# Four of sixteen attention tiles of each group transposed by VectorE and device memory instead of TensorE

## The reference

```python
q, k, v = (proj(Wq), proj(Wk), proj(Wv))
scores = jnp.einsum('bhsd,bhtd->bhst', q, k) * scale
scores = jnp.where(mask[None, None, :, :], -jnp.inf, scores)
attn = jax.nn.softmax(scores, axis=-1)
out = jnp.einsum('bhst,bhtd->bhsd', attn, v)
out = out.transpose(0, 2, 1, 3).reshape(B, S, E)
out = out @ Wo.T
rms = jnp.sqrt(jnp.mean(out * out, axis=-1, keepdims=True) + EPS)
xn = out / rms * rms_scale
...
xn = xn * (1.0 + sc[:, None, :]) + shift[:, None, :]
...
x = x + _L0_cond_ref(x, mask_SxS_bk1, cond_256, ...)
x = x + _L1_cond_ref(x, cond_256, L1_cond_q_right, L1_cond_spectral_gate)
```

## Time and profile before

| what | value |
| --- | --- |
| median of three runs | 858.3 us (858.19 to 858.86) |
| span of the profiled execution | 855.4 us, so 2.9 us less than the median |
| TensorE busy | 846.5 us (99%) |
| VectorE busy | 628.7 us (73%) |
| ScalarE busy | 615.9 us (72%) |
| GpSimd busy | 482.5 us (56%) |
| chain that ended last | PE 97%, DVE 1%, issue 1%, ACT 1% |

### The profile page before, as it was taken

How to read it: one execution, slowest core, us unless ns; L and a number is a source line. 1 busy time by engine, 2 the same in 40 slices (tenths; PEclk the granted TensorE clock), 3 DMA queues, 4 the chain that set the end, 5 groups by cost and what they waited for, 6 DMA issues and landing times.

```text
span 855.4 us, 17179 instructions
## 1 busy us (share of the span) xinstructions
PE 846.5 (99%) x5344; PEld 640.8 (75%) x5344; DVE 628.7 (73%) x1524; ACT 615.9 (72%) x1504; POOL 482.5 (56%) x346
## 2 busy tenths in 40 slices
PE   9999999999999999999999999999999999999997
PEld 6788888888887777767777677776777767777774
DVE  5521321322338899999999999999999999999886
ACT  6232332232329899999999999999999999999882
POOL 0999990000000111666777667776677766777794
PEclk9999999999999999999999999999999999999999
DMA  8854644654599658786687775788668777569201
GB/s 288 339 212 164 233 172 184 220 185 183 182 284 272 138 112 231 173 203 147 149 204 162 157 207 135 156 185 209 143 148 204 164 160 207 131 157 245 68 26 51
DMA packets 82355, 153.76 MB, mean 180 GB/s; under 512 B 8520, under 2 KB 9160, under 8 KB 82272
## 3 DMA queue, kind: packets, MB, share of 16 engines
q1 hardware_dynamic: 82128, 152.49, 65.8%
q10 hardware_dynamic: 144, 0.26, 0.1%
HBM read 102.35 MB, written 50.36 MB: 179 GB/s over the span
## 4 chain that ended last, share of the span: by engine, by line
PE 97%; DVE 1%; issue 1%; ACT 1%; POOL 0%; DVEq 0%; ACTq 0%
PE banks L788 26%; PE banks L120 14%; PE banks L816 13%; PE banks L851 10%; PE banks L471 9%; PE banks L473 9%; PE banks L472 9%; PE banks L797 2%; PE banks L831 1%; PE banks L456 1%; PE banks L444 0%; DVE probs L685 0%; ACT turned_probs L1013 0%; PE banks L510 0%; DVE banks L955 0%
## 5 line engine op out<-in xcount | busy, mean ns | idle before, releaser
L137 ACT ACTIVATE probs<-probs,least 128x512 f32<-128x512 f32 x512 | 363.4, 713 | 0.0
L129 DVE CUSTOM_DVE_ANT_0 probs<-banks,mask_bias 128x512 f32<-128x512 f32 x512 | 330.0, 681 | 37.5 <-PE banks L120 37.5
L788 PE MATMUL banks<-ident,probs 128*128 128x128 f32 x2048 | 306.4, 272 | 0.8 <-DVE turned_probs L901 0.7
L788 PEld LDWEIGHTS banks<-ident,probs 128*128 128x128 f32 x2048 | 252.6, 140 | 56.7 <-ACT probs L137 2.0
L120 PE MATMUL banks<-k_rows,q_rows 128*128 128x512 f32 x496 | 236.2, 478 | 0.0
L901 DVE COPY turned_probs<-banks 128x512 f32<-128x512 f32 x256 | 175.5, 686 | 2.3 <-PE banks L788 2.3
L400 DVE SCALAR_TENSOR_TENSOR late<-banks,late 128x512 fp32r<-128x512 f32 x64 | 43.9, 690 | 158.7 <-ACT late L337 158.7
L1013 ACT ACTIVATE turned_probs<-banks 128x512 f32<-128x512 f32 x256 | 147.1, 587 | 17.0 <-PE banks L788 13.5
L685 POOL TENSOR_TENSOR late<-rot,late 128x2048 f32<-128x2048 f32 x28 | 129.2, 4615 | 0.0
L337 ACT ACTIVATE late<-banks 128x512 fp32r<-128x512 f32 x64 | 38.2, 598 | 119.6 <-PE banks L473 112.5
L816 PE MATMUL banks<-turned_probs,v_sb 128*32 128x512 f32 (+1 forms) x1088 | 117.0, 570 | 1.3 <-ACT turned_probs L1013 1.3
(11 more groups left out here) (134 smaller groups left out, 1263.0 us busy)
## 6 DMA issues: line engine op xcount, KB each, us to landing
q_rows<-q_scratch SPq DMA_DIRECT2D x128, 256.0 KB, 6.1
k_rows<-k_scratch SPq DMA_DIRECT2D x124, 256.0 KB, 6.5
q_scratch<-late SPq DMA_DIRECT2D x64, 256.0 KB, 2.3
k_scratch<-late SPq DMA_DIRECT2D x64, 256.0 KB, 2.3
v_sb<-v_scratch SPq DMA_DIRECT2D x8, 1024.0 KB, 11.4
out<-late SPq DMA_DIRECT2D x29, 256.0 KB, 7.5
raw<-in_xT SPq DMA_DIRECT2D x7, 1024.0 KB, 5.4
v_scratch<-v_out SPq DMA_DIRECT2D x28, 256.0 KB, 2.0
```

Of the source, the lines that this page charges most:

```text
L129: dve.tensor_tensor_reduce(self.probs[:, n % RING, :], self.ps[:, n % SCORE_BANKS, :], self.mask_bias[:, c, :], 1.0, 3e38, ALU.add, ALU.mi ...
L137: act.activation(self.probs[:, n % RING, :], self.probs[:, n % RING, :], ACT.Exp, bias=self.least[:, n % 32:n % 32 + 1], scale=-1.0, accum ...
L788: last = pe.transpose(turn_bank("tile", n)[:, j * P:(j + 1) * P], probs[:, n % RING, j * P:(j + 1) * P], ident[:, :])
```

## The change

The four tiles of head 0 (places 0 to 3) of each whole group are no longer turned by TensorE. VectorE transposes their 32 x 32 blocks from `probs` into a new tile `blocks` (`block`, at places 0 to 3). SyncE writes `blocks` to device memory in four DMAs of 256 KB, each from 32 partitions, and reads them back in four DMAs, each into 128 partitions of `turned_probs` (`move_blocks`). The first of the four products of each part of `values` reads and writes in a pattern of 32 columns. The moves of the other twelve tiles are dealt out anew: 8 to ScalarE, as before, 4 to VectorE instead of 8. `rescale` and `residual` of VectorE become one step, which reads the projected chunk, the factor and the gain, and GpSimd gets a new step `add`. q and k pieces are loaded into every fourth partition. The ring `probs` has 10 places instead of 12, the `MASKS` and `EXPS` tables stay.

```diff
-RING, SLOTS = 12, HG + 1
+RING, SLOTS = 10, HG + 1
...
+BLOCK_PLACES = (0, 1, 2, 3)
+BLOCKS_AT = (0, 1, 2, 3)
...
-BY_ACT = {'early': '0101010101010101', 'whole': '0101010101010101', 'half': '01010011'}
+BY_ACT = {'early': '----101101101101', 'whole': '----101101101101', 'half': '01010011'}
...
-RESIDUAL = {(m + NG + 1, 1 if m < CHUNKS - 3 else 3): m for m in range(CHUNKS - 1)} | {(V - 1, 6): CHUNKS - 1}
...
     def load_q(self, sp, u, r):
-        sp.dma_start(f32(self.q[r * D:(r + 1) * D, u % 2]),
+        sp.dma_start(f32(self.q[r::HG, u % 2]),
...
-        if n >= RING:
-            dve.wait_ge(self.turned, n - RING + 1)
+        if n >= RING and BY_ACT[n - RING] == "-":
+            dve.wait_ge(self.blocked, n - RING + 1 - TURNS[n - RING + 1])
+        elif n >= RING:
+            dve.wait_ge(self.turned, TURNS[n - RING + 1])
...
+            def move_blocks(v):
+                sp.wait_ge(blocked, TC * (v + 1))
+                if v >= 2:
+                    sp.wait_ge(moved, 16 * TC * (v - 1))
+                for a in (0, 2, 1, 3):
+                    sp.dma_start(scr["blocks"][v % 2, a].rearrange("(k p) t -> p k t", p=D),
+                                 blocks[a * D:(a + 1) * D].rearrange("p k j c t -> p k (j c t)")).then_inc(blocks_out[a], 16)
+                if v >= 2:
+                    sp.wait_ge(valued, v - 1)
+                for a in (0, 2, 1, 3):
+                    sp.wait_ge(blocks_out[a], 16 * (v + 1))
+                    sp.dma_start(turned_probs[:, HG * v % SLOTS, a, :], scr["blocks"][v % 2, a]).then_inc(moved, 16)
...
+                if chunks == ALL:
+                    move_blocks(v)
                 if u + 2 < U:
                     load_unit(u + 2)
...
-                    last = pe.matmul(value_ps[i * D:(i + 1) * D, cols], v_sb[:, b % 2, part, h * D:(h + 1) * D],
-                                     turned_probs[:, (HG * u + i) % SLOTS, part, cols],
+                    to, of = value_ps[i * D:(i + 1) * D, cols], turned_probs[:, (HG * u + i) % SLOTS, part, cols]
+                    if i == 0 and chunks == ALL:
+                        if part == 0:
+                            pe.wait_ge(moved, 16 * TC * (v + 1))
+                        to = to.rearrange("p (c a t) -> p a c t", c=TC, a=TC)
+                        of = turned_probs[:, HG * u % SLOTS, :, part * P:(part + 1) * P].rearrange(
+                            "p a (c t) -> p a c t", c=TC)
+                    last = pe.matmul(to, v_sb[:, b % 2, part, h * D:(h + 1) * D], of,
                                      start=(part == 0), stop=(part == TC - 1))
...
-                turn(n)
+                if BY_ACT[n] != "-":
+                    turn(n)
...
+            def block(n):
+                v, u, i, c = ORDER[n]
+                dve.wait_ge(exped, n + 1)
+                if n == 0:
+                    dve.wait_ge(projected, (TC + 2 * NG) * (B - 1) + 2 * NG)
+                for a in range(TC) if c == 0 and v > 0 else ():
+                    dve.wait_ge(blocks_out[a], 16 * v)
+                dve.transpose(blocks[:, :, :, c, :].rearrange("p k j t -> p j k t"),
+                              probs[:, n % RING, :].rearrange("p (j k t) -> p j k t", j=TC, k=TC)).then_inc(blocked, 1)
...
-                dve.tensor_tensor(scaled[:, :], y_of(m), mod[:, b % 2, E:], ALU.mult).then_inc(scaled_ready, 1)
-
-            def residual(m):
-                c = m % TC
-                dve.wait_ge(scaled_ready, m + 1)
                 dve.wait_ge(rstd_ready, m + 1)
-                dve.wait_ge(shifted, m + 1)
-                dve.scalar_tensor_tensor(x_of(m), scaled[:, :], rstd[:, c % 2:c % 2 + 1], x_of(m),
-                                         ALU.mult, ALU.add).then_inc(summed, 1)
+                if m >= 2:
+                    dve.wait_ge(stored[c % 2], 16 * (m // 2))
+                dve.scalar_tensor_tensor(acc[:, c % 2], y_of(m), rstd[:, c % 2:c % 2 + 1], mod[:, b % 2, E:],
+                                         ALU.mult, ALU.mult).then_inc(scaled_ready, 1)
...
+                if chunks_of(v) == ALL and t in BLOCKS_AT:
+                    block(FIRST[v] + BLOCK_PLACES[BLOCKS_AT.index(t)])
...
+            def add(m):
+                pool.wait_ge(scaled_ready, m + 1)
+                pool.wait_ge(shifted, m + 1)
+                pool.tensor_tensor(x_of(m), x_of(m), acc[:, m % 2], ALU.add).then_inc(summed, 1)
...
+                if v > NG:
+                    rms(v - NG - 1)
                 if 0 < v <= POOL_GROUPS:
                     spread_inverse(v - 1)
                 if v > NG:
-                    rms(v - NG - 1)
+                    add(v - NG - 1)
```

More of the change, by code:

```diff
@@ L32, with tiles_of_group @@
 V = len(GROUPS)
-ORDER = [(v, u, i, c) for v, (u, chunks) in enumerate(GROUPS) for i in range(HG) for c in chunks]
+BLOCK_PLACES = (0, 1, 2, 3)
+BLOCKS_AT = (0, 1, 2, 3)
+def tiles_of_group(chunks):
+    tiles = [(i, c) for i in range(HG) for c in chunks]
+    if chunks == ALL:
+        blocked, tiles = tiles[:TC], tiles[TC:]
+        for place, tile in zip(BLOCK_PLACES, blocked):
+            tiles.insert(place, tile)
+    return tiles
+ORDER = [(v, u, i, c) for v, (u, chunks) in enumerate(GROUPS) for i, c in tiles_of_group(chunks)]
 SIZE = [HG * len(chunks) for _, chunks in GROUPS]
@@ L603, in attention @@
         turned_probs = sb("turned_probs", [P, SLOTS, TC, S])
+        blocks = sb("blocks", [P, TC, TC, TC, D])
         inv = sb("inv", [P, HG, TC])
@@ L631, in attention @@
         valued, normed = sem("valued"), sem("normed")
+        blocks_out = [sem(f"blocks_out{a}") for a in range(TC)]
+        moved = sem("moved")
         o_hi_ready, o_ready = sem("o_hi_ready"), sem("o_ready")
@@ L689, in attention @@
         rows.last_k = values_and_k[:, 0]
-        late_mix = [probs[:, 4 * j:4 * j + 4, :] for j in range(3)]
+        late_mix = [probs[:, 4 * j:4 * j + 4, :] for j in range(2)] + [blocks[:, :, :, :, :].rearrange(
+            "p k j c t -> p k (j c t)")]
+        late_junk = probs[:, RING - 1, 0:E // 2].bitcast(BF16)
         late_out = [turned_probs[:, 3, j, :] for j in range(3)]
@@ L984, in _ @@
                     split_lo(v - 1)
-                if not by_act(n - 1) and n > 0:
+                if n > 0 and BY_ACT[n - 1] == "0":
                     move_out(n - 1)
```

64 lines of the change are left out of this document (33 added, 31 removed).

## The result

The changed kernel takes 901.93 us (median of four runs, 901.3 to 902.49) against 858.25 us of the kernel before: a ratio of 1.0511, with a 95% interval of 1.0497 to 1.0526. It is slower by 5.1%. The forecast was 900.

What follows compares the result with a forecast made beforehand. TensorE sets the pace, with ScalarE's own list also closing the 17.82 us period. Whole groups add 39.0 and 3.0, so 855.4 + 42 = 897, plus 2.9 around it: 900 us; own range 880 to 912, 8 in 10 874 to 936.

Steps and rivals of the forecast that it cites:

- The pace: Whole groups: two transposes before `norm` delay mask 9, exponential 9 and moves 4 and 6; period 19.32 us against 17.82.
- side case without the transposes in the way: Whole groups, transposes at nothing: mask 9 ready at 6.8, exponential 9 at 7.55, turn 6 at 8.3, period 18.1 us.
- about 2 us before the value products: TensorE in whole groups: a wait of about 2 us before values, ended by ScalarE's last move.
- The rest of the period: ScalarE from move 6 on: 7 exponentials, single and paired moves and the square, 9.16 us, no mask or turn late.
- 26 x 1.50 + 3 x 1.0: Added time of whole groups: 1.50 us each for groups 4 to 29, 1.0 each for groups 1 to 3; +42 us.
- 17.5 us is the least that a period could take: ScalarE in whole groups: 16.6 us of work plus the 0.86 us wait before `inv_T`.
- 0, bounded by 1.4 us: Group 0 and the four half groups: no added time, bounded by group 0's four turns, 1.4 us either way.
- `rescale`'s wait for `rms`: VectorE: waiting for GpSimd's `rms` costs nothing, as VectorE waits for score 8 anyway, about 2.6 us after the change.
- Block transposes: VectorE: 0.60 us each, like a copy; rival 1, twice that (1.2): period 20.5, +78, 936 us, chance 0.10.
- The cover in the changed kernel: Blocks through device memory: last read lands at 16.1, values need them at 19.5, so 3.4 us of cover.
- one to two us over the period at worst: q and k loads, if at 205 GB/s: 10 us instead of 5, DMA total 20 us; case then dropped.
- Faster: Rival 3, whole groups: exponential 9 before 7.25, no wait before move 6; ScalarE's 17.5 us period, -10, 848 us, chance 0.11.

Runs made afterwards that it cites:

- each half of it, undone alone: On the changed kernel, either all block transposes moved ahead of mask 8 (867.15 us), or the blocked tiles spread to places 0, 2, 4, 6 (871.57 us).
- both parts undone: Changed kernel with all block transposes ahead of mask 8 and blocked tiles at places 0, 2, 4, 6: 849.38 us, ratio 0.9912 to the kernel before.
- the two runs without blocks: Changed kernel with all sixteen tiles turned by TensorE again: 861.92 us; the same with the residual again in VectorE's two steps: 857.35 us.
- a mean period of 16.90 us: Kernel with all transposes ahead of mask 8, blocked tiles 0, 2, 4, 6, and exponential 7 moved ahead of `inv_T`: 840.45 us, ratio 0.9800.
- the run with spread tiles: Changed kernel with blocked tiles at places 0, 2, 4, 6 instead of 0 to 3, transposes left where they were: 871.57 us, ratio 1.0170.

## Why the prediction was right, and where it was off

**The pace.** Right. The prediction put score 8, mask 8, mask 9 and exponential 9 at 4.21, 4.90, 7.32 and 8.06 in the period, and the trace has them at 4.20, 4.90, 7.31 and 8.04. Moves 4 and 6 were put at 7.07 and 10.16 with waits of 0.68 and 0.69 before them; they stand at 7.10 and 10.18, with 0.61 each. The experiments show the cause, in that each half of it, undone alone, gives 1.2 us per period. The prediction's side case without the transposes in the way, exponential 9 at 7.55, is what the run with all transposes ahead of mask 8 has: 7.54. TensorE's idle time came out in another place than it said: not about 2 us before the value products but 0.64 there, 1.00 before score 12, 0.47 before turn 15 and 0.28 before score 11.

**The rest of the period.** 9.16 us from move 6 on was too much: from 516.48 to the next group's exponential 2 at 525.41 it is 8.93. The square takes 0.57 (505.25 to 505.82), and I had taken 0.68, which is the distance from the square to the move behind it less that move's wait. The two pairs of moves take 1.02 and 0.96 instead of 1.05 each. So the term "26 x 1.50 + 3 x 1.0" was mis-sized: it measured 26 x 1.24 + 3 x 1.09 = 35.4 us, not 42. The same error is in "17.5 us is the least that a period could take": with both parts undone the period is 17.12, of which 0.81 is the wait before `inv_T`, so ScalarE's own work is 16.3 us and not 16.6.

**What was costed at nothing.** Group 0 and the half groups "0, bounded by 1.4 us" was wrong, and made up for the term before. The first value product is 3.9 us later: it waits 2.48 us for the blocks of group 0, and TensorE had stood 1.36 us for a mask before that (265.20). The half groups and the end cost 5.7 us; the two runs without blocks show that 4.6 us come from the single residual step, and what the other 1.1 us are stays open. I had placed `rescale`'s wait for `rms` in a stretch where VectorE waits anyway, which holds in whole groups. In a half group GpSimd, whose list is longer than the group, is late, and VectorE stands there with the next projection behind it. That the total came within 2 us of the forecast is in part luck: -6.6 and +9.6, and -1.1 for what lies around the span. The profiled execution of the changed kernel took 902.23 us with a span of 900.4, so 1.8 us and not 2.9; other runs of the kernel before have 1.8 as well (858.0 with a span of 856.2), so the one whose span was taken was about 1.1 us shorter than the median. The strided value product, costed at nothing, did cost nothing: 3.57 us from its start to `turn_scale` (506.52 to 510.09), against 3.58 before (612.89 to 616.47).

**Block transposes.** Right: 0.62 from start to start, taken as 0.60. Two places of the Trainium skill were weighed there. The trace agrees with section 3.8 of Vector Engine (DVE) Microarchitecture Reference (one element per cycle and lane): 512 columns take 696 ns, as long as a copy of them (686). The 311 ns that VectorE: DVE Perf Modes, section The three transpose paths, gives for 128 x 128 in bf16, paid four times, would be 1.24 us, an estimate that these 696 ns rule out.

**Device memory.** The cover in the changed kernel held: from group 1 on no value product waits for a DMA. It was not large, since at a mean period of 16.90 us seven of 29 do. The figure for q and k in 32 neighbouring partitions, "one to two us over the period at worst", is what that run gave: the mean of its 29 periods is 20.32 us, 1.28 above the changed kernel's 19.04, a part of it by the lower clock, which the sum did not have. My expectation for the run itself, nothing, went against my own sum. The rule of the Trainium skill on the DMA port swizzle (SBUF, State Buffer, Door 1), by which every fourth partition reaches all 16 ports and 32 neighbours only 8, agrees with the fall of the DMA share from 0.99 to 0.83 at more GB/s, 265 instead of 257.

**The rivals.** "Faster" needed exponential 9 before 7.25 and no wait before move 6. In the changed kernel neither was so (8.04, and 0.61 us). The kernel with both parts undone has exponential 9 at 7.35 and no wait before a move, and is faster. So the rival was nearly a true statement about another order of the same work; its bound of 7.25 was worked out with the 9.16 us that were too long.

## What to carry to other kernels

Here, with three engines within 7% of one another, the order in the lists counted for more than the work taken off one of them. Walk one period from the one instruction that everything waits for, with start-to-start times, before moving anything; it gave the period to 1.5% (19.32 for 19.05), though the change of the period only to a fifth (1.50 for 1.24). Put a new step where its engine already waits (here ahead of mask 8), and look whether the steps that went away had been filling another engine's wait. Walk the first and the last, shorter groups too, since a cover in the steady state need not be there.

## What the runs showed of the hardware

I had not expected the clock to matter. With the doubled transpose at place 3, a wait of TensorE of 1.75 us for mask 9 was followed in 13 of 29 periods by a little over 3 us at a granted clock of 0.50, the lower of the two levels (1.2 instead of 2.4 GHz), and those periods were about 1.6 us longer (21.41 against 19.85); in the other 16 the same wait left the clock at 1.00. In the changed kernel, with waits of 1.00 us there, the clock stayed at the upper level through all whole groups. The timeline of TensorE in the kernel with the doubled transpose at place 3, score 12 in both groups:

```profile
491.42 0.58 PE L134 MATMUL banks<-k_rows,q_rows 128*128 128x512 f32 x1 [1.75 <-DVE least L145]
...
512.82 0.50 PE L134 MATMUL banks<-k_rows,q_rows 128*128 128x512 f32 x1 [1.76 <-DVE least L145]
```

The score in the first group takes 0.58 us instead of 0.50. What decides between the two groups stays open. The clock fell to 0.50 as well around the 3.95 us of waiting before the first value product of the run with spread tiles, and did not around the changed kernel's 2.48 us at the same place. But in the run with the doubled transpose at place 1 it fell around a wait of 2.10 us in group 0 (score at 265.62, which took 0.80 us). So the length of the wait alone doesn't tell. From the table by stretches of 2 us of the run with spread tiles:

```profile
280.00:282.00 2.00, 2.00 (x15) 0.45 (x9) 0.00 (x0) 0.00 (x0) 0.00 (x0) 0.50 1.03 338
```

A block transpose on VectorE of 128 x 512 in 32 x 32 blocks took about as long as a copy out of the accumulators, 696 against 686 ns. Value products of which a fourth read and write in runs of 32 columns took as long as before, 3.57 against 3.58 us. How long the DMAs took depended on the partitions that they went to: the same q and k pieces landed in 7.5 and 8.4 us (medians) in 32 neighbouring partitions and in 4.6 and 4.7 us in every fourth one, in otherwise the same kernel.
